# First layer's expert results: scattered by rank and token by GpSimd per tile, loaded by chunk by SyncE, in place of a linear store and a gather

## The reference, cut to what matters

```python
x = x + attention0(layernorm(x), ctx)
x = x + shared(xn) + moe0(xn)          # xn = layernorm(x)
x = x + attention1(layernorm(x), ctx)
x = x + moe1(layernorm(x))
# moe0: 16 experts, the best two by logit, gates = sigmoid(logit)
moe = sum(gates[n, i] * (silu(g) * u) @ down_w[sel[n, i]] for i in (0, 1))
# moe1: 8 experts of width 1024, relu, two softmax weights
```

## Time and profile before

| | |
|---|---|
| median of 3 runs | 919.97 us (919.43 to 921.38) |
| profiled execution, first to last instruction | 917.2 us |
| mean granted TensorE clock | 0.961 |
| PE busy, share of the span | 811.1 us, 88% |
| DVE, ACT, POOL busy | 591.5, 401.2, 213.6 us |
| POOL's indirect DMAs | 47 gets and 32 gathers in layer 0, 39 gets and 39 puts in layer 1 |

### The profile page before, as it was taken

How to read it: one execution, slowest core, us unless ns; L and a number is a source line. 1 busy time by engine, 2 the same in 40 slices (tenths; PEclk the granted TensorE clock), 3 DMA queues, 4 the chain that set the end, 5 groups by cost and what they waited for, 6 DMA issues and landing times.

```text
span 917.2 us, 23713 instructions
## 1 busy us (share of the span) xinstructions
PE 811.1 (88%) x8698; PEld 602.5 (66%) x8699; DVE 591.5 (64%) x1391; ACT 401.2 (44%) x768; POOL 213.6 (23%) x185
## 2 busy tenths in 40 slices
PE   4879999799979999985689999998979999999994
PEld 3545555465648888853344666656449999999993
DVE  3345778768956677724565788869965555555562
ACT  3243556554232333320332666666874444444440
POOL 0004000100013333257012000001023444444432
PEclk9989999999999999997797999999999999999997
DMA  8865431305363333366235523229533333343331
GB/s 267 131 83 63 64 101 31 132 16 191 107 223 102 97 109 102 100 125 139 39 46 70 72 95 119 69 70 326 160 124 60 63 70 65 68 71 65 65 59 24
DMA packets 74593, 91.32 MB, mean 100 GB/s; under 512 B 15520, under 2 KB 60448, under 8 KB 74528
## 3 DMA queue, kind: packets, MB, share of 16 engines
q1 hardware_dynamic: 59600, 63.09, 28.3%
q0 software_dynamic: 13008, 25.97, 12.3%
q10 hardware_dynamic: 1920, 1.34, 0.5%
HBM read 60.86 MB, written 17.56 MB: 86 GB/s over the span
## 4 chain that ended last, share of the span: by engine, by line
PE 68%; DVE 12%; issue 8%; ACT 5%; DMA 3%; another core or an unknown queue 2%; SPq 1%; POOLq 0%; DVEq 0%; ACTq 0%
PE bank L955 18%; PE bank L968 14%; PE bank L717 5%; PE bank L862 3%; PE bank L738 3%; PE bank L686 3%; PE bank L578 3%; PE bank L534 3%; PE bank L940 3%; PE bank L874 2%; DVE neg_max L1458 2%; PE bank L549 2%; PE bank L704 2%; DVE arena L1755 2%
## 5 line engine op out<-in xcount | busy, mean ns | idle before, releaser
L968 PE MATMUL bank<-arena 128*128 x1218 | 279.4, 273 | 4.0 <-DVE arena L1768 2.2
L1326 ACT ACTIVATE arena<-bank,router_b 128x128 f32<-128x128 f32 x312 | 86.8, 375 | 124.0 <-DMA router_b<-in_exp_b 109.2
L1458 DVE TENSOR_REDUCE neg_max<-bank 128x2 f32<-128x512 f32 (+1 forms) x180 | 117.5, 685 | 28.5 <-PE bank L686 28.3
L968 PEld LDWEIGHTS bank<-arena 128*128 128x128 f16 x1218 | 119.0, 98 | 11.9 <-issue 10.3
L955 PE MATMUL bank<-att,arena 128*128 128x128 f16 x960 | 104.6, 219 | 2.7 <-issue 2.7
L1156 ACT ACTIVATE arena<-bank 128x1024 f32<-128x1024 f32 x96 | 96.7, 1026 | 15.7 <-PE bank L704 15.0
L955 PE MATMUL bank<-attT,arena 128*128 128x128 f16 x912 | 99.3, 219 | 0.0
L955 PE MATMUL bank<-arena 128*128 128x128 f16 x1128 | 97.2, 222 | 2.0 <-DVE arena L1760 2.0
L955 PEld LDWEIGHTS bank<-att,arena 128*128 x960 | 91.8, 98 | 8.7 <-issue 3.3
L1938 POOL DMA_INDIRECT out<-arena,put_i x39 | 65.9, 1691 | 110.2 <-DVE arena L1781 96.1
L955 PEld LDWEIGHTS bank<-attT,arena 128*128 x912 | 86.5, 98 | 5.6
(11 more groups left out here) (216 smaller groups left out, 1359.8 us busy)
## 6 DMA issues: line engine op xcount, KB each, us to landing
arena<-arena SPq DMA_DIRECT2D x96, 128.0 KB, 4.8
arena<-in_exp_up SPq DMA_DIRECT2D x16, 512.0 KB, 3.7
y_d<-arena SPq DMA_DIRECT2D x47, 128.0 KB, 1.7
arena<-in_exp_dn SPq DMA_DIRECT2D x5, 1024.0 KB, 6.0
arena<-in_exp_up SPq DMA_DIRECT2D x5, 1024.0 KB, 5.1
arena<-in_exp_b SPq DMA_DIRECT2D x39, 128.0 KB
arena<-in_ctxT SPq DMA_DIRECT2D x8, 512.0 KB, 7.1
arena<-in_exp_dn SPq DMA_DIRECT2D x16, 256.0 KB, 4.0
```

The costliest lines, as they stand in the source:

```text
L968: last = mm(yP[u], hidT[u][x][:, k], weights(e, 1, w, k * D, D), start=n == 0, stop=n == n_second - 1)
L1326: last = fn(hid[:, k * P:(k + 1) * P], upP[u][:, half, (k % 4) * P:(k % 4 + 1) * P], ACT.Relu, bias=b1_col[u][:, k:k + 1], scale=1 / WS)
L1458: v.tensor_reduce(neg_max[u][:, column(m * HM):column(m * HM) + 2 * HM - 1:2], mx[m % 2].rearrange("p (h k) -> p h k", h=HM), AX.X, ALU.ma ...
```

## The change

Two indirect `put`s replace two things: SP's linear stores and POOL's gathers.

- `y_d` has 6144 + 4096 rows. POOL's `put(i)` in layer 0 writes tile i's 128 rows to `put_i`: rank 0's result of token n to row 6144 + n, rank 1's to 6144 + 2048 + n. Padding slots get a row of their own below 6144 (`own_row`, one more operation at the program's start). There is no addition and no bounds check in it. It stands behind `get(i + 5)` in POOL's list, as in layer 1.
- POOL's wait for `dn_mm` goes; its fill of `far` stands behind the last `put`.
- SP has no stores in layer 0. After the `far` copies it waits for all puts, then loads chunk by chunk with two plain DMAs of 512 KB each; chunks 0 and 1 stand ahead of `keys(1, 0)`, chunks 2 and 3 behind it and ahead of `keys(1, 1)`, each after the chunk two before has landed.
- VectorE waits for 2 landings a chunk, not 8; its work is the same.

```diff
-        y_d = dram("y_d", (NS[0] * P, D), F32)
+        y_d = dram("y_d", (TOKENS + 2 * N, D), F32)
...
                 if l:
+                    for u in range(RESULTS[0]):
+                        sp.wait_ge(B[0]["y_stored"][u], (NS[0] + RESULTS[0] - 1 - u) // RESULTS[0] * 16)
+                    load_results(0)
+                    load_results(1)
                     keys(1, 0)
+                    load_results(2)
+                    load_results(3)
                     keys(1, 1)
...
-            def store_results():
+            def load_results(c):
                 s = B[0]
-                for i in range(NS[0]):
-                    sp.wait_ge(s["y_ready"], i + 1)
-                    sp.dma_start(y_d[i * P:(i + 1) * P], y_rows[i % 4]).then_inc(s["y_stored"][i % 4], 16)
+                after(sp, s["gathered"][c % 2], c // 2 * 2 * 16)
+                for i in range(2):
+                    sp.dma_start(y_got[c][:, i], by_token(y_d[TOKENS + i * N:TOKENS + (i + 1) * N], c)).then_inc(s["gathered"][c % 2], 16)
...
-                v.tensor_scalar(pad[0][:, 0:S], tile_of, 0.0, pcol[:], ALU.is_equal, ALU.mult)
+                v.scalar_tensor_tensor(out=pad[0][:, 0:S], in0=tile_of, scalar=0.0, in1=own_row[:, 0:S], op0=ALU.is_equal, op1=ALU.mult)
...
+            v.tensor_scalar(own_row[:], iota_s, float(P), pcol[:], ALU.mult, ALU.add).then_inc(once["iota_ready"], 1)
...
-                if l:
-                    gather_results()
...
                 def put(i):
                     pool.wait_ge(s["y_ready"], i + 1)
+                    if l == 0:
+                        pool.indirect_dma_start(y_d, bass.IndirectOffsetOnAxis(ap=put_i[:, i:i + 1], axis=0),
+                                                y_rows[i % 4], None).then_inc(s["y_stored"][i % 4], 16)
+                        return
...
-                for i in range(S + BEHIND if l else S):
+                for i in range(S + BEHIND):
                     if i < S:
                         get(i)
-                    if l and i >= BEHIND:
+                    if i >= BEHIND:
                         put(i - BEHIND)
...
-                    pool.wait_ge(s["dn_mm"], S)
                     pool.memset(far, SHIFT).then_inc(once["far_set"], 1)
```

More of the change, by code:

```diff
@@ L207, in xattn_moe_program @@
         pad = [sb(f"pad{l}", [P, 48]) for l in range(2)]
+        own_row = sb("own_row", [P, 48])
         at_f = sb("at_f", [P, 48])
@@ L517, in _ @@
                     load_context(1, 0, NC)
-                    store_results()
                 else:
@@ L1829, in combine @@
                 dve.wait_ge(once["gates_ready"], l + 1)
-                dve.wait_ge(s["gathered"][g % 2], (g // 2 + 1) * 2 * TC * 16)
+                dve.wait_ge(s["gathered"][g % 2], (g // 2 + 1) * 2 * 16)
                 for i in range(2):
@@ L1848, in _ @@
             v.tensor_copy(inv_val[:, :, 1], iota_b[:, TOKENS // P:TOKENS // P + 2 * T]).then_inc(once["iota_ready"], 1)
-            dve.wait_ge(once["iota_ready"], 4)
+            v.tensor_scalar(own_row[:], iota_s, float(P), pcol[:], ALU.mult, ALU.add).then_inc(once["iota_ready"], 1)
+            dve.wait_ge(once["iota_ready"], 5)
             for l in range(2):
@@ L1878, in _ @@
         def _(pool):
[L1879 to L1889, removed]
             pool.memset(far, SHIFT).then_inc(once["far_set"], 1)
```

## The result

The changed kernel takes 929.69 us (median of 4 runs, 928.59 to 930.83) against 919.7 (917.67 to 921.38): a ratio of 1.0093 with an interval of 1.0052 to 1.0133. A later comparison with more runs of both gave 1.0091 (1.0067 to 1.0115). The forecast was 894.0, in a range of 887 to 908, so it missed by 36 us and with the wrong sign. The profiled execution has a span of 927.0 us, against 917.2.

What follows compares the result with a forecast made beforehand. PE bounds layer 0's experts; between the layers POOL's 32 gathers leave PE a hole. Gap -27.5, experts +1.2 and small edits +0.3 give -26.0 us: span 891.2, plus 2.8 to the median, 894.0, range 887 to 908.

Steps and rivals of the forecast that it cites:

- Gap, -27.5 us: Between the layers: without POOL's gathers, DVE's keys 2 starts at 416.5 instead of 443.71; gain 27.5 us, bounds 20 to 28.5.
- ACT's keys 2 behind the first key stack: In the gap: the stack's DMAs queue behind chunk loads, ACT done at 415.6, 0.9 us before DVE asks; next to be late.
- Price of a put, 1.00 us: Layer 0's experts: an indirect put occupies POOL 1.00 us, like the get; 0.95 to 1.70 kept for the range.
- Experts, +1.2 us: Layer 0's experts: puts make POOL the pace by 0.03 us a step over 41 steps, +1.2 us.
- POOL's cycle: Layer 0's experts: put, get and two 0.30 us gaps take POOL 2.56 us against PE's step of 2.53.
- the get's delay: Layer 0's experts: behind the put, the get's rows land at 4.76 us, needed at 5.06; costs nothing at the median.
- Rival A: Layer 0's experts: a put costing 1.70 us makes POOL the pace, 29.9 us lost, 922.7 in all; chance 13%.
- B: Layer 0's experts: a put of 1.15 to 1.5 us loses 7 to 22 us, 900 to 915; chance 9%.
- C: In the gap: traffic, not the gathers, holds ACT; keys 2 comes 12 us later than forecast, 906; chance 10%.
- D: In the gap: only DVE's 10.7 us wait shrinks, to 3.5; its 14.4 us wait stays; 914; chance 3%.
- Small edits, +0.3: At the program's start and elsewhere: `own_row` with its wait and another small edit cost 0.3 us together at most.

Runs made afterwards that it cites:

- e1: The changed kernel with SyncE storing layer 0's results in order of tiles, no put on GpSimd, and the chunk loads reading those rows: 891.55 us.
- e10: The kernel before with its 32 indirect gathers between the layers made plain loads on GpSimd's queue: 898.29 us beside 920.83.
- e7: The changed kernel with only odd tiles put by GpSimd, even ones stored by SyncE, chunk loads reading another buffer: 911.98 us.
- e4: The changed kernel with each layer 0 put made a plain GpSimd DMA of the 128 rows: 896.93 us.
- e14: The changed kernel with layer 0's get made a plain GpSimd load, the puts still indirect: 892.91 us.
- e13: e1 with its get made plain too, so no indirect DMA in layer 0's steps: 892.78 us.
- e2: e1 with a GpSimd fill of 128x512, no DMA, in the place of each put: 899.4 us.
- e8: e1 with 32 indirect gathers on GpSimd added between the layers, into a buffer that nobody reads: 891.46 us.
- e5: The changed kernel with layer 0's put six tiles behind the get, not five: 924.39 us.
- e3: e1 with a second indirect get of the same 128 rows, unused, in the place of each put: 928.81 us.
- e11: e3 with the extra get fetching 32 rows instead of 128: 926.14 us.

## Why the prediction was wrong

- **Gap, -27.5 us: right.** Measured -28.0 between the traces and -26.4 in e1. By its steps, counted from the last result out of PSUM (394.54, now 430.56): combine 0 at +9.7 was +9.2, keys 1 at +13.1 was +14.0, keys 2 at +22.0 was +22.6, and from there to the last maximum 39.7 was 38.5. That they sum up so well is in part luck, +0.6 and -1.1. What was late next was not what the prediction had named, ACT's keys 2 behind the first key stack, but ACT's keys 1, which waited 2.35 us for PE's product and let DVE wait 1.48 us; keys 2 came without a wait of DVE. The reason for the gain, that the holds are the gathers', is borne out by e10.
- **Price of a put, 1.00 us: right** (0.993 median, 1.05 mean).
- **Experts, +1.2 us: the step that failed; it was 34 from the first get to the last result.** "POOL's cycle: 1.00 + 0.30 + 0.96 + 0.30 = 2.56 us against the step of 2.53" counts what a DMA costs the engine that issues it, and "the get's delay" what it costs the one that waits for its rows. Neither counts what it costs PE, DVE and ACT, which have nothing to do with it. e7 leaves POOL time to spare and pays 0.78 us for each put; e4 and e14 keep POOL's share just as high and lose 0.3 and 0.7 us in that stage.
- **Rival A** had the place and the sign, and a time 7 us too short (922.7), but not the reason: it needed a put of 1.63 us. "Right" as to sign would have been luck. B falls with the put's price. C falls with the gap after, where the DMA share is 0.64, above the 0.61 of before, and ACT waits 2.35 us at the longest for a keys product of PE once keys 0 are in; the longer ones there are for values 0 (4.67, as before), for DVE (4.2) and for the last queries (4.4). D falls with the 28.0 us.
- **The row that spoke** was there. The prediction said of ACT's holds in the gap that "each of these holds lies inside the gathers", booked their end as the gain of taking 32 indirect DMAs away, and then added 47 of the same kind to a stage where PE was busy 95 of 100 us, at no such price. With the gap's own rate, 27.5 / 32 = 0.86 us each, the sum would have been -27.5 + 47 x 0.86 = +12.9, 932.9 us: 3 above the measured time. So close a hit would have been luck. That rate also holds 6 us by which the first chunk came later, which is no hold, and it would charge the get that is alone in its step as well, which costs nothing (e13); the trace of before couldn't say that.
- **Small edits, +0.3:** too small to be told apart in the runs.

Shown: the loss comes with a second indirect DMA per step, of either direction, of 32 or 128 rows, and not with a plain one; POOL doesn't run out of time in e7 and pays all the same. Not tested: an operation on POOL that is no DMA and as long as the put (the fill of e2 was 0.53 us and cost 6 us). Inferred: that it is TensorE's signals that are held, since the ends of matmuls in the records are modelled, and the sight of DVE and ACT starting together (336.8) is what speaks for it; ACT's start at 332.92 says that it is no plain gate. Open: what in the DMA does it, whether indirect DMAs that stand apart would cost less, and why the 32 gathers of e8, which nobody waits for, cost 3 us at most, where those of before cost about 20 beside their landing.

## What to carry to other kernels

An engine with time to spare is not a free place for a DMA: where a profile shows other engines held beside a kind of DMA, carry a price for it along when the same kind is moved to a stage in which everyone waits for TensorE at short notice. Count indirect DMAs per step of a pipeline, not their bytes; here one was free, and each second one cost 0.70 to 0.78 us (0.61 in pairs with a pause between them, e5). Before giving rows an order on the way out, ask whether that takes more indirect DMAs (47 tiles with padding) than fetching them in order (32) did.

## What the hardware showed that I had not expected

- An indirect DMA takes GpSimd 0.96 us for 128 rows and 0.87 for 32 (medians of the extra get in e3 and e11). A plain one of the same 128 KB takes 0.55 to 0.59, and one of 512 KB 0.80 in the mean (the eight that keep the normalised input).
- DVE waited 57 us in total for nothing that the profile could name (285 to 440 us; in e3, which keeps SP's stores, 56.8 from 285 to 430). Idle time of that kind on one engine can be the trace of a DMA on another.
- The kernel before took 905.6 us in one comparison, on one chip, and 919 to 923.5 in all the others. Two other kernels' traces from there show no stage outside the gap that is faster; why the gap was shorter is open.
